# Relative-position attention on one core: the second stage gathers the split query and key stacks from the parts, instead of reading stacks stored by the first

## The reference, cut to what matters

```python
def _L0_attn_b_ref(hidden_states, Wq, bq, Wk, bk, Wv, bv, dist_emb, Wo, bo, ln_gamma, ln_beta):
    # H = 16 heads of D = 8 columns, B = 8, S = 512
    q = heads(hidden_states @ Wq + bq)
    k = heads(hidden_states @ Wk + bk)
    v = heads(hidden_states @ Wv + bv)
    scores = jnp.einsum('bhqd,bhkd->bhqk', q, k)
    dist_idx = pos_l - pos_r + M - 1
    pos_emb = dist_emb[dist_idx]
    rel_q = jnp.einsum('bhld,lrd->bhlr', q, pos_emb)
    rel_k = jnp.einsum('bhrd,lrd->bhlr', k, pos_emb)
    scores = (scores + rel_q + rel_k) / jnp.sqrt(jnp.asarray(D, scores.dtype))
    probs = jax.nn.softmax(scores, axis=-1)
    ctx = jnp.einsum('bhqk,bhkd->bhqd', probs, v)
    ...
```

## Time and profile before

| what | us |
|---|---|
| median of the three runs | 4912.55 |
| the profiled execution, its own time | 4912.15 |
| span of its trace, first to last instruction | 4910.4 |
| stage one of the second attention, from the trace | 2234 to 3058 |
| stage two, from the trace | 3058 to 3980 |
| PE, DVE, ACT, POOL busy over the span | 3915, 2890, 2635, 1690 |

### The profile page before, as it was taken

The page is one execution under the profiler, slowest core; times in us unless marked ns, Lnnn a source line. Parts: engine busy times, 40 slices in busy tenths (PEclk is TensorE's granted clock), DMA queues, the critical chain, the costliest instruction groups (busy, mean ns, idle before and its releaser), DMA issues.

```text
span 4910.4 us, 102424 instructions
## 1 busy us (share of the span) xinstructions
PE 3915.1 (80%) x31924; PEld 2380.9 (48%) x31924; DVE 2889.9 (59%) x6305; ACT 2635.3 (54%) x6550; POOL 1689.6 (34%) x1383
## 2 busy tenths in 40 slices
PE   2999999999488888734666565999999945888886
PEld 1555555554255555522222222677777723555554
DVE  2555555555577777543444443566666665777775
ACT  1555555554367777523333333566666624777774
POOL 0000000000588888523222222111111116878774
PEclk9999999999799999965555555999999977999998
DMA  3222222221111111027999999777777711111111
GB/s 118 87 78 78 78 78 80 81 78 53 49 25 23 27 27 23 17 71 293 380 381 385 380 381 369 269 262 260 248 272 250 256 43 52 25 26 25 25 23 32
DMA packets 374686, 701.06 MB, mean 143 GB/s; under 512 B 54180, under 2 KB 161016, under 8 KB 374568
## 3 DMA queue, kind: packets, MB, share of 16 engines
q1 hardware_dynamic: 330536, 565.25, 33.6%
q0 software_dynamic: 44032, 134.30, 7.4%
HBM read 336.53 MB, written 314.64 MB: 133 GB/s over the span
## 4 chain that ended last, share of the span: by engine, by line
PE 51%; DMA 13%; DVE 10%; issue 9%; POOL 7%; ACT 4%; SPq 2%; DVEq 1%; POOLq 0%; ACTq 0%
DMA rel_k<-b_stage_k 12%; PE ps L332 5%; PE ps L1465 5%; PE ps L340 5%; PE ps L351 5%; PE ps L1474 5%; PE ps L1456 3%; PE ps L1485 3%; DVE f_rs L1028 2%; POOL f_rn L758 2%; PE ps L866 2%; DVE f_rc L1025 2%; POOL f_rot L756 2%; PE ps L1357 2%; DVE b_stage_k L1381 2%
## 5 line engine op out<-in xcount | busy, mean ns | idle before, releaser
L1381 DVE COPY b_stage_k<-ps 128x640 f32<-128x640 f32 (+2 forms) x512 | 359.1, 722 | 469.6 <-DMA rel_k<-b_stage_k 410.3
L430 ACT ACTIVATE a_p<-a_s,a_min 128x512 f32<-128x512 f32 x512 | 366.0, 715 | 470.3 <-DVE a_min L474 470.3
L1378 ACT ACTIVATE b_stage_q<-ps 128x640 f32<-128x640 f32 (+2 forms) x512 | 316.0, 624 | 505.4 <-PE ps L1360 388.0
L474 DVE CUSTOM_DVE_ANT_0 a_s<-ps,a_table 128x512 f32<-128x512 f32 x512 | 333.5, 689 | 374.5 <-PE ps L332 371.9
L1539 ACT ACTIVATE c_p<-c_s,c_min 128x512 f32<-128x512 f32 x512 | 370.2, 723 | 290.7 <-PE ps L1474 180.3
L1357 PE MATMUL ps<-b_e,b_st_k 48*128 48x512 bf16 (+1 forms) x512 | 305.9, 597 | 261.1 <-DVE b_stage_k L1381 261.1
L1574 DVE CUSTOM_DVE_ANT_0 c_s<-ps,c_rq 128x512 f32<-128x512 f32 x512 | 352.8, 689 | 200.8 <-PE ps L1465 188.1
L188 POOL COPY y<-ln_rows 128x512 f32 x32 | 19.9, 621 | 1304.8 <-DVE ln_rows L180 1304.8
L949 ACT ACTIVATE f_p<-f_s,f_min 128x128 f32<-128x128 f32 x1024 | 396.3, 390 | 89.1 <-DVE f_min L1014 88.7
L756 POOL TENSOR_TENSOR f_rot<-f_rc,f_rs 128x1024 f32<-128x1024 f32 x128 | 302.9, 2367 | 255.6 <-DVE f_rs L1028 255.3
L758 POOL TENSOR_TENSOR f_rn<-f_ss,f_power 128x16 f32<-128x16 f32 x128 | 373.8, 2920 | 14.9 <-DVE f_ss L1037 1.4
(11 more groups left out here) (171 smaller groups left out, 9194.5 us busy)
## 6 DMA issues: line engine op xcount, KB each, us to landing
rel_q<-b_stage_q SPq DMA_DIRECT2D x64, 1280.0 KB, 7.8
rel_k<-b_stage_k SPq DMA_DIRECT2D x64, 1280.0 KB, 7.7
c_rq<-rel_q SPq DMA_DIRECT2D x64, 1024.0 KB, 7.7
c_rk<-rel_k POOLq DMA_DIRECT2D x64, 1024.0 KB, 11.9
a_table<-skew_bias SPq DMA_DIRECT2D x64, 896.0 KB, 4.6
f_vb<-f_v SPq DMA_DIRECT2D x256, 128.0 KB, 2.4
rel_k<-b_stage_k SPq DMA_DIRECT2D x32, 1024.0 KB, 9.5
rel_q<-b_stage_q SPq DMA_DIRECT2D x32, 1024.0 KB, 5.3
```

Of the source, the lines that this page charges most:

```text
L430: nc.scalar.activation(a_p[:, lt % 2, h, :], a_s[:, lt % 2, h, :], ACT.Exp, bias=a_min[:, lt % 2, h:h + 1], scale=-1.0, accum_out=a_sum[:, ...
L1381: moves_b1(dve, 1, lambda out, src: nc.vector.tensor_copy(out, src))
```

## The change

Stage one no longer stores the stacks to DRAM. The tensor `stack_qk`, its semaphore, the two stores and the holds on them go. Stage two builds its stack in `c_st` as stage one does, with twelve gathers from `split_qk`, ahead of the four loads of `rel_k`; all count on the same semaphore, whose awaited value rises from 80 to 256 a unit of a buffer.

```diff
@@ sync_b1_loads
         def step(u, q, i):
-            hold(pool, b_st_stored[q], i * 32 + 32)
             hold(pool, b_rel_full[0], u * 16 + 16)
             hold(pool, b_rel_full[1], u * 16 + 16)
@@ sync_b1
         def step(u, q, i):
-            hold(sp, b_st_loaded[q], i * 192 + 192)
-            for n in range(2):
-                sp.dma_start(stack_dram[u, n], b_st[n][:, q, :, :]).then_inc(b_st_stored[q], 16)
             for lt in range(LT):
...
         for n in range(2):
-            sp.wait_ge(b_st_stored[n], 32 + 32 * (UNITS_B // 2))
@@ pool_b2
             hold(pool, c_scored, u * TILES + 16)
-            pool.dma_start(c_st[:, q, :, :, :].rearrange("p n h t -> p n (h t)"),
-                           stack_dram[u].rearrange("n p h t -> p n (h t)")).then_inc(c_loaded[q], 16)
+            for n in range(2):
+                for g in range(6):
+                    at = (n * 3 + SPLIT_ORDER[n][g]) * (P * SEQ)
+                    src = bass.AP(split_dram.tensor, (u // QB) * (6 * P * SEQ) + (u % QB) * (QB * DB * SEQ) + at,
+                                  [[SEQ, DB], [DB * SEQ, QB], [1, SEQ]])
+                    pool.dma_start(c_st[DB * g:DB * g + DB, q, n, :, :], src).then_inc(c_loaded[q], 16)
             for rt in range(LT):
@@ tensor_b2, scores
             if a == 0:
-                pe.wait_ge(c_loaded[q], (u // 2) * 80 + 80)
+                pe.wait_ge(c_loaded[q], (u // 2) * 256 + 256)
```

More of the change, by code:

```diff
@@ L1113, in program @@
     split_dram = nc.dram_tensor("split_qk", [BATCH, 2, 3, P, SEQ], BF16).ap()
-    stack_dram = nc.dram_tensor("stack_qk", [UNITS_B, 2, STACK, QB, SEQ], BF16).ap()
     rel_dram = [nc.dram_tensor("rel_q", [BATCH, LT, HB, P, WIN], F32).ap(),
@@ L1297, in program @@
     b_st_loaded = [sem("b_st_loaded0"), sem("b_st_loaded1")]
-    b_st_stored = [starting("b_st_stored0", 32), starting("b_st_stored1", 32)]
     b_rel_full = [starting("b_relq_full", 32), starting("b_relk_full", 32)]
```

## The result

The changed kernel takes 4852.85 us in the median of four runs (4846.60 to 4862.17), the kernel before 4911.51 us: a ratio of 0.9883, 95% interval 0.9865 to 0.9900, so 58.7 us or 1.2% faster. The forecast was 4848 us, range 4830 to 4888.

What follows compares the result with a forecast made beforehand. Stage one was taken as bound by DMA bytes, stage two by PE with DMA hidden. From the profiled 4912.15 us, minus 65.5 for the stores, plus 1 for the start of stage two, gave 4847.7, say 4848 us; range 4830 to 4888.

Steps and rivals of the forecast that it cites:

- Stage one is bound by bytes: Stage one of the second attention: DMA share 1.02 at 382 GB/s, so a byte taken out is time.
- the hole: Inside a stage-one unit: four microseconds at 290 GB/s, put down to the 48-partition stores, losing 1.15 us beyond their bytes.
- The price of the two stores: Stage one: bytes 0.97 us plus 1.15 us lost rate, 2.1 us a unit, 65 us over 31 units.
- Rival 1: Stage one: only the stores' bytes come off and the slow stretch moves to the next transfer; 4881 us, chance 0.20.
- The small holes: Stage-one units: short drops in rate and DMA share, 0.5 us a unit in the mean, expected to stay.
- The loop through the staging buffer: Stage one: DVE's wait for stores to land sets 22.3 us a unit, close to the new unit but not deciding.
- Rival 2: Stage one: the loop through the staging buffers holds the unit and nothing is gained; 4915 us, chance 0.09.
- The start of stage two: Before PE's first scores: the twelve gathers replacing one load delay the start, taken as +1 us.
- the gathers (0.39 MB) keep DMA busy 9.3 us at 410 GB/s: Start of stage two: c_rq's 3.41 MB and the gathers fill DMA from some 3060.5 to 3069.8 until c_rk comes.
- The bounds -1.4 and +6.7: Start of stage two: 1.4 us gained if the slow stretch there closes, 6.7 us lost if POOL's whole delay shows.
- Steady units of stage two, 0 us: Stage two: POOL's queue grows 6.7 us a unit, covered by its 7.35 us wait for PE, so 0 us.
- Rival 3: Stage two: the gathers come late and PE waits for loads every unit; 5325 us, chance 0.04.

Runs made afterwards that it cites:

- e3: The changed kernel with two 192 KB stores a unit put back in SP's queue, from 128 partitions in 1.5 KB rows: 4879.12 us, 0.9933 of the kernel before.
- e6: The changed kernel with the two 192 KB stores a unit put back from 48 partitions, each 4 KB row cut into 1 KB pieces: 4921.87 us, one run.

## Why the prediction was right

*Stage one is bound by bytes*: right. With 4% of the bytes and the hole gone, the stage went from 802.1 to 734.3 us and nothing took the place of DMA; the share stays at 1.03 to 1.04.

*The price of the two stores, 2.1 us a unit, 65 us*: right, 67.8 us measured, and e3 splits it as the text did: 0.98 us a unit of bytes (predicted 0.97), and the rest, 67.8 - 31.4 = 36.4 us or 1.14 a unit, for the hole (predicted 1.15). That it fits to the hundredth is luck: one followed unit gave the forecast, and with the other profiles of both kernels the 67.8 lie anywhere from 63.5 to 69.2. Rival 1, bytes only, falls all the same. The attribution of the hole to the 48-partition shape is shown by e3 against e6. The other half of that sentence, that the gathers make none, holds for stage one but for some 0.5 us a unit, and not for the start of stage two.

*The small holes*: I let half a microsecond of them stand. They closed, and 0.5 us at the tail of the gathers took their place, so the unit is 23.2 us as forecast, in this part by chance. That the stores had pushed the engines out of step, so that some ran dry early, would explain it; no run here tests it.

*The loop through the staging buffer, 22.3 us*: not contradicted; the unit stopped at 23.2 with the DMA engines full. Rival 2 falls.

*The start of stage two, +1 us*: this term was mis-sized; it is +4.0 (26.11 against 22.16; the four starts with the one load lie at 22.2 to 23.7, all with the gathers in the old order at 25.4 to 26.2). The step that failed is "the gathers (0.39 MB) keep DMA busy 9.3 us at 410 GB/s" together with rel_q. In that stretch rel_q's tail and the gathers moved at 271 GB/s for 8 us, a loss of 8 x (410 - 271)/410 = 2.7 us, where the hole of the kernel before had lost 1.4. The second hole, 3 us at 192 GB/s while the gathers of unit 1 (the last six issued from 3016.06 on) were under way too, loses 1.6. The rest is bytes: from memset to PE's first scores DMA moves 26.11 us x 298 GB/s = 7.78 MB instead of 22.16 x 331 = 7.34, so 1.1 us more at 410. These make 2.7 - 1.4 + 1.6 + 1.1 = 4.0 us. The bounds -1.4 and +6.7 held it.

*Steady units of stage two, 0 us*: right. The cover that the text named was used up to 0.46 us. Rival 3 falls: a gather lands while the next is issued, and the last c_rk arrives before PE asks.

*The sum*: by the stretches 67.8 - 4.0 = 63.8 us should come off, against 64.5 forecast. The medians say 58.7, and 60.5 when it was run again. The 3 to 5 us between are no more than the stages that the change does not touch vary from one execution to the next (3180 to 3198 us). The total came nearer than its terms: stage one gave 2.3 us more than forecast and the start cost 3 us more, and the two cancel.

## What to carry to other kernels

In a stage that is bound by DMA, look at the rate microsecond by microsecond inside one period: a transfer that holds the engines while the rate falls costs more than its bytes, and removing it gives both back. Stores from 48 partitions were such here; where such a store can't be removed, try its bytes from 128 partitions, which here made as many bytes cost half. Work that is hidden in every period but the first shows at the first, so cost the start of a stage by itself, and order its loads by who waits for them.

## What the runs showed of the hardware that was not expected

The price of 0.393 MB of stores a unit, beside a saturated queue, was 0.98 us from 128 partitions, 1.19 from 64, 1.38 from 96, 2.1 to 2.2 from 48, and 2.58 from 48 in both halves. The Trainium skill, SBUF — State Buffer, section Door 1: The DMA port swizzle, says that the rate of a DMA hangs on how many of the memory's sixteen ports its partitions reach, and that partitions 0 to 63 reach eight of them. By that rule 64 partitions should cost as much as 48, and 96 less than either. The costs don't agree, at least beside other traffic, and with one profile each from 128, 64 and 96: 64 cost little over the bytes, 96 more than 64, and 48 in both halves the most. The packets agree in part: those of the stores from 64 partitions are slowed (175 ns against 121), those from 128 are not.
